# Local attention: the mask added by VectorE as it takes the scores out of PSUM, not written into the score banks by TensorE

## What is computed

```python
def local_attention(q, k, v):              # per head; w = 32
    bk2, bv2 = (look(bk), look(bv))        # each window sees itself and the one before
    mask = (it < jb) | (it > jb + w) | (jb == -1)
    sim = jnp.einsum('bhwie,bhwje->bhwij', bq, bk2) * QK_SCALE
    sim = jnp.where(mask, -jnp.finfo(sim.dtype).max, sim)
    attn = jax.nn.softmax(sim, -1)
    return jnp.einsum('bhwij,bhwje->bhwie', attn, bv2)
```

## Time and profile before

| | |
|---|---|
| median of 3 runs | 4785.16 us (4783.14 to 4789.26) |
| the profiled execution | 4791.83 us, of which the span is 4789.8 us |
| mean granted TensorE clock, share of full | 0.927 |
| TensorE busy, share of the span | 4238.3 us, 88% |
| VectorE | 3247.4 us, 68% |
| ScalarE | 2600.4 us, 54% |
| GpSimd | 2418.3 us, 50% |

### The profile page before, as it was taken

How to read it: one execution, slowest core, us unless ns; L and a number is a source line. 1 busy time by engine, 2 the same in 40 slices (tenths; PEclk the granted TensorE clock), 3 DMA queues, 4 the chain that set the end, 5 groups by cost and what they waited for, 6 DMA issues and landing times. The chain is left out here.

```text
span 4789.8 us, 167679 instructions
## 1 busy us (share of the span) xinstructions
PE 4238.3 (88%) x70890; PEld 3371.5 (70%) x70890; DVE 3247.4 (68%) x5510; ACT 2600.4 (54%) x4233; POOL 2418.3 (50%) x1949
## 2 busy tenths in 40 slices
PE   6997899999999999999999999999997749658667
PEld 5885777777777777777777777777775439558447
DVE  4445777777777777777777777777775564564554
ACT  2231566665666666666666666666664317546435
POOL 2123655656565566555565666555652037516025
PEclk9777999999999999999999999999998959868878
DMA  0000322222222322222222222222221021222022
GB/s 25 0 0 30 88 67 65 64 80 67 69 67 62 86 66 69 64 80 69 69 64 80 68 64 70 64 69 69 69 64 36 0 61 50 67 61 62 7 63 75
DMA packets 214200, 281.53 MB, mean 59 GB/s; under 512 B 58878, under 2 KB 103716, under 8 KB 212740
## 3 DMA queue, kind: packets, MB, share of 16 engines
q1 hardware_dynamic: 203972, 251.85, 19.9%
q0 software_dynamic: 9536, 19.55, 1.5%
HBM read 54.88 MB, written 18.28 MB: 15 GB/s over the span
## 5 line engine op out<-in xcount | busy, mean ns | idle before, releaser
L1541 POOL TENSOR_TENSOR local_normed<-local_rot,local_sines 128x512 f32<-128x512 f32 x768 | 953.8, 1276 | 818.4 <-PE local_bank L1266 813.9
L1551 POOL TENSOR_TENSOR local_normed<-local_normed,local_inv_norm 128x1024 f32<-128x1024 f32 x384 | 732.8, 1929 | 276.1 <-ACT local_inv_norm L1441 276.1
L1618 DVE TENSOR_TENSOR local_rot<-local_bank,local_table 128x1024 f32<-128x1024 f32 x384 | 470.3, 1225 | 409.2 <-ACT local_squares L1422 402.6
L1186 PE MATMUL local_bank<-local_wqkv_hi,local_ys_hi 128*128 128x512 f32 x1152 | 496.8, 431 | 28.4 <-issue 17.4
L1417 ACT COPY local_v_tile<-local_bank 128x1024 f32<-128x1024 f32 x192 | 195.1, 1016 | 548.0 <-PE local_bank L1188 548.0
L1618 DVE TENSOR_TENSOR local_sines<-local_bank,local_table 128x1024 f32<-128x1024 f32 x384 | 466.4, 1215 | 0.0
L1624 DVE TENSOR_REDUCE local_norm<-local_squares 128x16 f32<-128x1024 f32 x384 | 464.0, 1209 | 0.0
L1188 PE MATMUL local_bank<-local_wqkv_hi,local_ys_lo 128*128 128x512 f32 x1152 | 458.8, 398 | 0.0
L1187 PE MATMUL local_bank<-local_wqkv_lo,local_ys_hi 128*128 128x512 f32 x1152 | 456.5, 396 | 0.0
L1422 ACT ACTIVATE local_squares<-local_bank 128x1024 f32<-128x1024 f32 x384 | 396.9, 1034 | 78.7 <-PE local_bank L1188 78.7
L1605 DVE TENSOR_REDUCE local_top<-local_bank 128x16 f32<-128x1024 f32 x192 | 234.8, 1223 | 246.2 <-PE local_bank L1214 245.8
(11 more groups left out here) (421 smaller groups left out, 8957.0 us busy)
## 6 DMA issues: line engine op xcount, KB each, us to landing
local_vals<-local_v_tile SPq DMA_DIRECT2D x1152, 130.0 KB
local_vals<-local_v_tile SPq DMA_DIRECT2D x672, 65.0 KB
local_stage<-in_L_ffn_Wqkv SPq DMA_DIRECT2D x6, 1536.0 KB
moe_w<-y_rows SPq DMA_DIRECT2D x32, 256.0 KB, 4.9
moe_w<-in_L_ffn_W SPq DMA_DIRECT2D x3, 2048.0 KB, 9.9
x_rows<-moe_rows SPq DMA_DIRECT2D x12, 512.0 KB, 3.9
local_wo<-in_L_ffn_Wo SPq DMA_DIRECT2D x6, 512.0 KB, 9.0
moe_taken<-x_rows,moe_take POOLq DMA_INDIRECT x149, 2.6
```

The costliest lines, as they stand in the source:

```text
L1186: nc.tensor.matmul(out, hi, wqkv_hi[:, d0:d1], start=True, stop=False)
L1541: last = nc.gpsimd.tensor_tensor(of_heads(normed, a)[:, :, to], of_heads(rot, a)[:, :, to], of_heads(sines, a)[:, :, of], ALU.add)
L1551: nc.gpsimd.tensor_tensor(of_heads(normed, a), of_heads(normed, a), inv_norm[:, a * HEADS:(a + 1) * HEADS].unsqueeze(2).to_broadcast([P, H ...
L1618: last = nc.vector.tensor_tensor(of_heads(out, a), src, table[:, m % TILES, row, :].unsqueeze(1).to_broadcast([P, HEADS, HD]), ALU.mult)
```

## The change

VectorE gets the mask `band` (f32, 128 x 64, one for a sequence's first tile and one for the others) in a new first step of `centre`: it reads the score banks, adds the mask broadcast over the heads, and writes `scores` in SBUF. The maximum and the subtract then read `scores`, no longer the banks, and the subtract works in place. A semaphore `masked` orders the add before the maximum. The wait for `probs_turned` of the tile before, which guards `scores`, now stands ahead of the add. TensorE's two mask products and the tiles `band8` and `ident16` go, every score product has `start=True`, and `pads_ready` is waited for at 1.

```diff
-        band8 = sb("band8", [P, 2, CH, WIN], BF16)
-        ident16 = sb("ident16", [P, P], BF16)
...
-                    "max_ready": 1, "centred": 1, ...
+                    "masked": 1, "max_ready": 1, "centred": 1, ...
...
-                pe.wait_ge(pads_ready, 2)
+                pe.wait_ge(pads_ready, 1)
...
-                    for odd in range(2):
-                        nc.tensor.matmul(bank[:, SCORES[odd], :], ident16[:], band8[:, min(t, 1)].rearrange("p h k -> p (h k)"),
-                                         start=True, stop=False, skip_group_check=True)
                     for c in range(CH):
                         for b in range(BLOCKS):
                             for odd in range(2):
...
-                                                        start=False, stop=True, skip_group_check=True, tile_position=(HD * odd, b * BLOCK))
+                                                        start=True, stop=True, tile_position=(HD * odd, b * BLOCK))
...
-                act.wait_ge(pads_ready, 2)
+                act.wait_ge(pads_ready, 1)
...
-                nc.vector.tensor_copy(ident16[:], g.ident[:])
-                nc.vector.tensor_copy(band8[:], band[:].unsqueeze(2).to_broadcast([P, 2, CH, WIN])).then_inc(pads_ready, 1)
...
                 def centre(m):
                     src = bank[:, SCORES[0]:SCORES[1] + 1, :].rearrange("p a (c k) -> p a c k", k=WIN)
+                    rows = scores[:].rearrange("p c a k -> p a c k")
                     dve.wait_ge(q["scores_done"], tile("scores_done", m))
-                    nc.vector.tensor_reduce(top[:], src, AX, ALU.max).then_inc(q["max_ready"], 1)
+                    dve.wait_ge(q["probs_turned"], tile("probs_turned", m - 1))
+                    nc.vector.tensor_tensor(rows, src, band[:, min(m % TILES, 1)].unsqueeze(1).unsqueeze(1).to_broadcast([P, 2, CH, WIN]),
+                                            ALU.add).then_inc(q["masked"], 1)
+                    dve.wait_ge(q["masked"], tile("masked", m))
+                    nc.vector.tensor_reduce(top[:], rows, AX, ALU.max).then_inc(q["max_ready"], 1)
                     dve.wait_ge(q["max_ready"], tile("max_ready", m))
-                    dve.wait_ge(q["probs_turned"], tile("probs_turned", m - 1))
-                    nc.vector.tensor_tensor(scores[:].rearrange("p c a k -> p a c k"), src, top[:].unsqueeze(3).to_broadcast([P, 2, CH, WIN]),
+                    nc.vector.tensor_tensor(rows, rows, top[:].unsqueeze(3).to_broadcast([P, 2, CH, WIN]),
                                             ALU.subtract).then_inc(q["centred"], 1)
```

More of the change, by code:

```diff
@@ L1058, in body @@
                     "exp_done": 1, "v_copied": 1, "squared": 2, "probs_t_ready": 1, "qkt_copied": 2, "out_copied": 1,
-                    "max_ready": 1, "centred": 1, "qk_normed": 2, "products_ready": 2, "norms_ready": 2,
+                    "masked": 1, "max_ready": 1, "centred": 1, "qk_normed": 2, "products_ready": 2, "norms_ready": 2,
                     "sums_inverted": 2, "att_ready": 2, "y_added": 1,
@@ L1075, in body @@
                     "logs_ready", "inv_norms_ready")
-        DVE_MADE = ("max_ready", "centred", "products_ready", "norms_ready", "sums_inverted", "att_ready", "y_added",
+        DVE_MADE = ("masked", "max_ready", "centred", "products_ready", "norms_ready", "sums_inverted", "att_ready", "y_added",
                     "stats_ready", "aggregated", "var_ready", "shift_ready", "prod_ready", "seq_done")
```

## The result

| | before | after |
|---|---|---|
| median of 7 runs each, same chip | 4789.26 us (4783.14 to 4802.81) | 4820.04 us (4815.28 to 4831.22) |
| ratio, with its 95% interval | | 1.0065 (1.005 to 1.008) |
| span of the profiled execution | 4789.8 us | 4818.0 us |

The change makes the kernel slower by 31 us, 0.65%. The forecast was +8, so 4793; the time lies 2 us above the range of 4762 to 4818. The forecast's base, 4785, was the median of three runs; the median of seven is 4 us higher, so the change itself came out 23 us above what was forecast for it. Of the three directions slower had the largest chance (0.41).

What follows compares the result with a forecast made beforehand. The prediction took TensorE to bound the kernel, by share (88%). Its terms, -22 -2 +22 +8 -7 +9, summed to +8 us, so 4793 us on a base of 4785, with a range of 4762 to 4818.

Steps and rivals of the forecast that it cites:

- kind 0: First of every four tiles in a sequence (m mod 4): the later subtract eats TensorE's gain; -2 us over 48 tiles.
- kind 1: Second of every four tiles: VectorE stays hidden behind ScalarE's square, each gains 0.45 us; -22 us over 48 tiles.
- kind 2 with the seams: Third of every four tiles: exponential 0.52 us later, +22 us in 42 tiles; five layer seams cost 1.25 us each.
- kind 3: Last of every four tiles: +8 us in 19 not waiting for scores; -7 in the others, half the stall moving along.
- after the last score tile: Last two tiles: no square hides the subtract, so the exponential comes 1.25 us later in each; +3 us.
- ahead of the first: Start-up: two copies and the second pads_ready count go, but TensorE's first projection waits for something later; 0 us.
- turn-taking: The subtract, with two SBUF inputs, waits out GpSimd's running normalising product, then needs 1.08 us; mean near 1.7 us.
- rival 1: Subtract and GpSimd's product take no turns, as the second input is a repeated maximum; about -50 us, 4735; chance 0.08.
- Rival 3: Gap before the first small weight load stays without the mask products; kind 1 gains nothing, +30 us, 4815; chance 0.06.
- Rival 4: Denser TensorE issue makes 15 to 25 more tiles stall 1.76 us in the scores; +26 to +44 more, 4825; chance 0.06.

Runs made afterwards that it cites:

- run 1: Kernel after, but VectorE adds the mask in place in the score banks, so the subtract has one SBUF input; 4783.69 us against 4789.64, ratio 0.9984.
- run 2: Kernel before without the two mask products and without any mask, so TensorE's part alone; 4750.27 us, ratio 0.9917.
- run 7: Kernel before with two dummy products of the mask's width ahead of the masks in kind 3; 4792.85 us, ratio 1.0002.
- run 6: Mixed kernel: VectorE adds the mask in the score banks in kinds 0 and 1, TensorE writes it as before in kinds 2 and 3; 4757.0 us, ratio 0.9929.
- run 3: VectorE's part alone: TensorE still writes half the mask's value as in the kernel before, VectorE adds the other half in the new centring; 4831.18 us, ratio 1.0089.
- run 5: Kernel after with two dummy products as wide as the mask ahead of the scores in kind 3 alone; 4811.98 us against 4791.76, ratio 1.0048.

## Why the prediction was right, and where it was wrong

The terms of the sum beside what the profiled executions show (48 tiles each; kind 2 has its seams added, 22 + 6; of its measured 28.1, 3.5 stand in the last but one tile of all, which the forecast has in the row after the last score tile):

| term | forecast, us | measured, us |
|---|---|---|
| kind 0 | -2 | -0.3 |
| kind 1 | -22 | -16.9 |
| kind 2 with the seams | +28 | +28.1 |
| kind 3 | +8 - 7 | +23.0 |
| after the last score tile | +3 | -0.4 |
| ahead of the first | 0 | -5.1 |
| sum | +8 | +28.2 |

**Right: the turn-taking, so rival 1 is out.** The add is 1.22 us; the subtract waits for the rest of the running product and then needs 1.08 us more; the mean of 1592 ns lies near the 1.7 forecast, the longest, 2.45, a little above its 2.3. Run 1 shows that it is the second SBUF input. The Trainium skill (SBUF — State Buffer, section Who interferes with whom) has the rule that a VectorE instruction with two SBUF inputs contends with a GpSimd instruction that reads SBUF. The trace agrees, 1592 ns against 1224 in run 1, also for an input that is a repeated maximum, which was open before.

**Right: kinds 0 and 2, and the seams.** Kind 0's gain is eaten (16.13 us a tile against 16.20, medians). Kind 2 grows by 0.45 us (14.44 against 13.99) where the forecast had 0.52, and four of the five seams by 1.23 to 1.25, the fifth by 2.15.

**Right in mechanism, a little off in size: kind 1.** The exponential stays 5.40 us behind the first score load (5.39 before), so VectorE is hidden. But the saving is 0.35 us a tile, not 0.45. I took it that only 0.06 us were the small weight load waiting; the rows after show that load idle for 0.80 us where it had 0.42 behind a mask, so more of the wait stays when the mask goes. Ahead of kind 2, where run 2 finds 0.34 as well, the row at 2248.81 shows no such idle time, and what keeps the rest there stays open. Rival 3 was right for this third of the 0.52.

**Wrong: the stalled tiles of kind 3.** The failed step is this: "If the stall moves with TensorE each gains 0.52 (-15 us for 28); if it ends at a time set elsewhere, nothing. I take half: -7." The stop does end at a time set elsewhere, but that does not cost nothing. The tiles without a stop behaved (17.72 against 17.20, +0.52 each, 18 of them +9, forecast +8). The others were to bring 7 us and lost some 14. In them two things were missed, and they are what the sum was short by (kind 3 came out 22 us above its forecast, the whole sum 20).

First, the stop's end doesn't move with the work just ahead of it. The row of the prediction held a hint that I did not use: the stop has no releaser. From the numbers of loads issued before it one can see what it goes by. In the same tile it comes after 127 loads before, 95 after, 71 in run 7. Up to this tile the change removed 224 pairs of load and product (two a tile, 112 tiles), which is 32 short of twice 128, and 127 less 32 is 95. Run 7 added 56 pairs (two in each of 28 tiles), and 127 less 56 is 71. So the place of the stop is fixed by the count in TensorE's list, once in 128 pairs, 256 instructions. It is no matter of one tile: counted over all records of TensorE's queue (loads, products, semaphore waits), all 237 stops of kind 3 in the ten traces stand at the same remainder of 256, 28 or 29. And from the place one such count earlier to the end of the stop it is always about as long: the median over the stopped tiles is 4.2 us before, 4.1 after, 4.4 in run 7, 4.1 in run 1 and 4.0 in run 6. In kind 3 the scores follow close behind another 128 small pairs (L1287, the products with the probabilities; the row at 2327.22 has the last 33), so two such places come within this time. Time saved between them is then waited out at the second. What is done in that time the DMA view shows, with a queue called "instruction": first on the page of the kernel before (packets, MB, share):

```profile
q8 instruction: 545, 8.93, 0.8%
```

and then in the 0.1 us from 2316.9 us of the same kernel:

```profile
q8 instruction: 1, 0.02, 75.1%
```

Each packet has 16,384 bytes, and each such place has one. In this tile of the kernel before the packet starts at 2316.95, lands at 2318.15, and TensorE goes on 1.41 us later; after, it lands at 2329.70 and TensorE goes on 1.54 us later. All 262 stops in the score loads of the ten traces end 1.19 to 1.71 us after their packet has landed, and in 5013 of the 5014 places of the ten stages TensorE passes no earlier than 1.18 us after it. The packet of a stop starts 0.3 to 2.3 us after the place before has been passed, so its landing is tied to that place. That TensorE waits there for its own next 256 instructions follows from this and the queue's name; no run changed the queue.

Second, a longer stop costs clock. Six tiles before and 13 after have the clock at the 1.2 GHz level behind the stop, and such a tile takes 1.85 us more (20.31 against 18.46; 20.34 against 18.61 before): 7 tiles, +13 us. A stretch is 3.4 us long, so by estimate up to 1.7 us of the 1.85 are the clock and the rest is the longer stop. With the +9 of the others this makes 22 of the 23 measured. That the removed 0.5 us of TensorE work is the cause is shown from both sides: run 2 has the stretches without VectorE's part, run 3 has VectorE's part without them, run 5 puts the time back and they fall from 22 or 24 to 14, and run 7 adds more to the kernel before and they fall from 13 to 5. Why some stops of 2 us are followed by the low clock and others not, the runs don't settle; the table shows only that longer ones are more often.

**Rival 4 had the right place and the wrong mechanism.** It gave 4825, near the 4820 measured, by 15 to 25 more tiles that stop. There are 20 in the table where there were 19. They stop longer, and they are followed by the half clock. It would be wrong to count it as a hit.

**Where the gain of the change went.** TensorE's part alone brings 43 us in the stage, instead of some 90 for 192 masks of 0.45 to 0.52: the price was 0.34 in half of the tiles, and kind 3 gave back 13 and more. VectorE's part alone costs 34. Added up that is -8; together they give +34. The difference lies in kind 0 (+15), kind 2 (+24) and kind 3 (+6), with -3 in kind 1. In kinds 0 and 2 the subtract is last once VectorE has the mask (0.26 and 0.90 us in which the exponential waits for it, rows at 2222.14 and 2255.21), so what TensorE saves ahead of it isn't gained: it is spent waiting there. In kind 0 GpSimd's pair also stands 0.44 us later relative to the scores once the mask is gone (run 3). The prediction had the waiting; it took GpSimd's pair as fixed, and it had not the +13 of kind 3 in run 2.

## What to carry to other kernels

Before work is taken off the bounding engine, read what that engine waits for in each kind of tile. Here a stop without a releaser did not move, and time saved ahead of it bought only a longer stop, more often with a lower clock behind it. Where the waits name nothing, count the instructions between the stops and look at the DMA queues, the one for instructions too. When VectorE takes on work, keep one input of each large operation in PSUM where GpSimd runs beside it; here that alone was worth 47 us. Where tiles differ in their slack, choose the method by kind: the mixed kernel has 0.7% less time than before, where the uniform change has 0.65% more.

## What the runs showed of the hardware that was not expected

- In 5013 of 5014 cases TensorE passes the place that comes once in 256 instructions of its list no earlier than 1.18 us after the landing of a 16,384-byte packet of the queue "instruction"; the packet takes about 1 us. If TensorE gets there sooner it stops, with no semaphore involved; the end of the stop lies 3.6 to 4.9 us behind the place before in most stopped tiles. In these kernels this happens where two groups of 128 small loads and products, 1.5 us each, follow each other closely. A short distance between two places does not always bring a stop: where the packet was early, places only 1.2 to 3 us apart were passed without one.
- A stop of 2.2 to 2.4 us in the mean comes with 22 to 24 half-clock stretches in 3140 us, one of 1.8 to 1.9 us with 8 to 14, one of 1.5 us with 5. With 384 bf16 products fewer the mean clock of the whole execution fell from 0.927 to 0.923. With 96 more (run 7) it is 0.930, which the runs of the kernel before beside it reach too (0.925 to 0.930).
- Two dummy products of 512 columns ahead of the scores of kind 3, where 22 of 48 tiles stop, cost nothing in sum (+0.4 us in the stage of run 7, which is within what two executions of one kernel differ by).
- A small weight load behind a large product sits idle for 0.80 us; with a mask product between them it is 0.42 us behind the mask.
